# One column of table rows a tile of a graph network, fetched row by row by SyncE and ScalarE in place of one gather

## The reference

```python
for l in range(L):
    ht = einsum('nd,rdo->nro', h, W_rel[l])             # a row for each node and relation
    h_rel = segment_sum(ht[src, etype], dst) + h @ W_loop[l] + b_rel[l]
    z = (h @ W_gat[l]).reshape(n, H, DH)
    e = leaky_relu(sum(z * attn_l[l], -1)[src] + sum(z * attn_r[l], -1)[dst], 0.2)
    ex = exp(e - segment_max(e, dst)[dst])
    alpha = ex / segment_sum(ex, dst)[dst]
    h_gat = segment_sum(alpha[:, :, None] * z[src], dst).reshape(n, D) + b_gat[l]
    hc = concatenate([h_rel, h_gat], 1) @ W_fuse + b_fuse
    if l == 0: hc = hc * sigmoid(concatenate([hc, mean(edge_weight)], 1) @ W_gate + b_gate)
    h = relu(hc)
return layernorm(x + h)
```

## Time and profile before

| | |
|---|---|
| median of the runs (3959.73 to 3967.59) | 3964.04 us |
| span of the profiled execution, first to last instruction | 3490.2 us |
| GpSimd busy | 2489.3 us, 71% |
| VectorE busy | 2380.3 us, 68% |
| TensorE busy | 689.4 us, 20% |
| ScalarE busy | 424.8 us, 12% |
| mean DMA traffic | 145 GB/s |

### The profile page before, as it was taken

The page is one execution under the profiler, slowest core; times in us unless marked ns, Lnnn a source line. Parts: engine busy times, 40 slices in busy tenths (PEclk is TensorE's granted clock), DMA queues, the critical chain, the costliest instruction groups (busy, mean ns, idle before and its releaser), DMA issues.

```text
span 3490.2 us, 18122 instructions
## 1 busy us (share of the span) xinstructions
PE 689.4 (20%) x1897; PEld 372.5 (11%) x1897; DVE 2380.3 (68%) x3226; ACT 424.8 (12%) x769; POOL 2489.3 (71%) x2642
## 2 busy tenths in 40 slices
PE   8942111222122230011121111221000000000000
PEld 5421000111011110000000000110000000000000
DVE  8536666677676764665777756674776788877786
ACT  3530110111111120101111111111000000000000
POOL 1457777777777756777777777775777777777776
PEclk9965555555655555555555555555555555555555
DMA  7774444455545544444454544454433333333332
GB/s 271 315 249 129 134 147 152 152 151 152 152 152 159 168 145 118 130 151 152 151 152 151 153 152 152 152 173 140 107 106 107 107 106 107 106 106 107 106 103 74
DMA packets 143244, 505.96 MB, mean 145 GB/s; under 512 B 44277, under 2 KB 51002, under 8 KB 133618
## 3 DMA queue, kind: packets, MB, share of 16 engines
q0 software_dynamic: 130032, 444.45, 43.4%
q1 hardware_dynamic: 13186, 61.24, 4.5%
HBM read 341.05 MB, written 164.51 MB: 145 GB/s over the span
## 4 chain that ended last, share of the span: by engine, by line
POOL 45%; issue 29%; DVE 10%; DMA 6%; PE 4%; POOLq 3%; DVEq 1%; ACT 1%; SPq 1%; ACTq 0%
POOL meta_nat L594 20%; POOL late L594 14%; POOL scratch L594 10%; DVE acc L1381 3%; PE ps_table L886 1%; DMA late<-table,stage_mid 1%; DMA table<-rows 1%; DMA scratch<-table,stage_tail 1%; DVE late L1377 1%; DVE scratch L1377 1%; DVE meta_nat L1377 1%; POOLq L369 1%; POOL table L671 1%; DMA meta_nat<-table,stage_head 1%; PE ps_cnt L919 1%
## 5 line engine op out<-in xcount | busy, mean ns | idle before, releaser
L594 POOL DMA_INDIRECT meta_nat<-table,stage_head x1200 | 1139.0, 949 | 395.7 <-issue 385.3
L594 POOL DMA_INDIRECT late<-table,stage_mid x720 | 681.9, 947 | 219.4 <-issue 217.9
L594 POOL DMA_INDIRECT scratch<-table,stage_tail x555 | 525.9, 948 | 175.5 <-issue 175.2
L1025 PE MATMUL ps_mix<-ident,hr 128*128 128x128 f32 x75 | 35.5, 473 | 1991.2 <-DVE hg L1401 1991.2
L788 ACT ACTIVATE ps_cnt<-logit 128x68 f32<-128x68 f32 x189 | 43.7, 231 | 2767.1 <-DVE logit L1363 2766.1
L1381 DVE TENSOR_REDUCE acc<-meta_nat 128x132 f32<-128x2112 f32 x75 | 290.6, 3875 | 8.1 <-DVE meta_nat L1377 0.5
L1371 DVE TENSOR_REDUCE acc<-meta_nat 128x128 f32<-128x2048 f32 x75 | 282.6, 3767 | 0.0
L1049 PE MATMUL ps_table<-wrel,hT 128*128 128x512 f32 x400 | 266.4, 828 | 0.0
L1353 DVE TENSOR_TENSOR raw<-late,er_cur 128x64 f32<-128x64 f32 x45 | 12.0, 267 | 324.5 <-DMA late<-table,stage_mid 324.5
L1025 PEld LDWEIGHTS ps_mix<-ident,hr 128*128 128x128 f32 x75 | 13.6, 182 | 2039.8 <-DVE hg L1401 2039.8
L1381 DVE TENSOR_REDUCE acc<-scratch 128x132 f32<-128x1188 f32 (+1 forms) x69 | 208.7, 3024 | 7.1
(11 more groups left out here) (237 smaller groups left out, 1701.4 us busy)
## 6 DMA issues: line engine op xcount, KB each, us to landing
table<-rows SPq DMA_DIRECT2D x25, 2080.0 KB, 7.7
meta_nat<-table,stage_head POOLq DMA_INDIRECT x1200, 2.8
late<-table,stage_mid POOLq DMA_INDIRECT x720
scratch<-table,stage_tail POOLq DMA_INDIRECT x555, 2.8
meta<-meta_ranked SPq DMA_DIRECT2D x1, 2438.0 KB, 15.1
wrel<-in_L_gnn_W_rel POOLq DMA_DIRECT2D x2, 1024.0 KB, 13.5
meta_nat<-in_x SPq DMA_DIRECT2D x1, 832.0 KB, 18.4
table<-rows,stage_id POOLq DMA_INDIRECT x50, 7.8
```

Source lines behind the costliest of these rows:

```text
L594: pool.indirect_dma_start(out=slots[b][:, k, :], out_offset=None, in_=table[l % 2], in_offset=bass.IndirectOffsetOnAxis(ap=index, axis=0)) ...
L1025: pe.transpose(mix[0], hr[:], ident[:])
```

## The change

For tiles 1 to 24 of each layer the first column of the lists (the first edge of each node) is no longer gathered by GpSimd. The lists are 82 long; `M_LIST` is where GpSimd's own list starts, one behind `M_ELL`. `tile_slots` is one less for these tiles (16 at least), starts are one more and counts one less.

The first column of all tiles is transposed by TensorE, multiplied by 260, stored as `lone_rows` in HBM (25 x 128 integers). In each tile SyncE loads 80 of the 128 places into its part of SBUF and ScalarE 48. Each loads them into registers, 16 at a time, and issues for each one DMA of 1040 bytes from the table to one partition of `lone_row` [128, 260], with the address from the register. VectorE, at the start of a tile, waits for all of them, copies `lone_row` into slot 0 of buffer H, and signals (`s_taken`) that `lone_row` may be written again; both issuers wait for that signal before the next tile's rows. VectorE's head group then takes slots 0 to 16 as new edges. SyncE runs its own loop over the tiles. ScalarE issues its 48 in three chunks: after the gate, after the second group's exponential, and after the evacuations of the next table. The buffer `yo` is placed in the room of the relation weights.

```diff
+LIST = ELL + 2
-    SCATTERED = M_ELL + ELL
+    M_LIST = M_ELL + 1
+    SCATTERED = M_ELL + LIST
+    BY_SP = 80
+    BY_ACT = P - BY_SP
+    LOADED = 16
+        lone_rows = dram("lone_rows", [T, P], I32)
+        lone_row = sb("lone_row", [P, ROW])
+        def fetch_lone(eng, l, places, at, lanes, landed, regs):
+            eng.reg_load(regs, places[0:1, at:at + len(regs)])
+            for reg, p in zip(regs, lanes):
+                place = eng.snap(reg, min_val=0, max_val=NULL * ROW)
+                eng.dma_start(lone_row[p:p + 1, :], table_flat[l % 2][:, bass.ds(place, ROW)]
+                              ).then_inc(landed, 16)
...
+            def lone_tile(l, t):
+                sp.dma_start(lone_sp[:], lone_all[:, bass.ds(t * P, BY_SP)]
+                             ).then_inc(s_at_sp, 16)
+                sp.wait_ge(s_taken, n_taken)
+                sp.wait_ge(s_at_sp, n_at)
+                sp.reg_add(n_at, n_at, 16)
+                sp.reg_add(n_taken, n_taken, 1)
+                for c in range(0, BY_SP, LOADED):
+                    fetch_lone(sp, l, lone_sp, c, range(c, c + LOADED), s_lone_sp, regs)
...
+            for l in range(L):
+                if l:
+                    sp.wait_ge(s_stored, 16 * (1 + l * T))
+                with sp.Fori(1, T) as t:
+                    lone_tile(l, t)
...
+            def lone_chunk(l, c):
+                if c == 0:
+                    act.wait_ge(s_at_act, n_at)
+                    act.reg_add(n_at, n_at, 16)
+                    act.wait_ge(s_taken, n_taken)
+                    act.reg_add(n_taken, n_taken, 1)
+                fetch_lone(act, l, lone_act, c * LOADED,
+                           range(BY_SP + c * LOADED, BY_SP + (c + 1) * LOADED), s_lone_act, places)
...
+                if lone:
+                    if first and l:
+                        act.wait_ge(s_stored, 16 * (1 + l * T))
+                    lone_chunk(l, 0)
                 with act.If(groups > 1):
                     group()
+                    if lone:
+                        lone_chunk(l, 1)
                     with act.If(groups > 2):
                         group()
+                with act.Else():
+                    if lone:
+                        lone_chunk(l, 1)
                 if not first:
                     next_rows(l, act.snap(n_last, min_val=0, max_val=T - 1))
                     act.reg_add(n_last, n_last, 1)
+                if lone:
+                    lone_chunk(l, 2)
...
+            pe.wait_ge(s_lone, 1)
+            pe.transpose(ps_cnt[0:T, 256:256 + P], lone[:], ident[:]).then_inc(s_lone_ps, 1)
...
+            v.tensor_scalar(tile_slots[:, 1:T], tile_slots[:, 1:T], -1.0, float(PAIR), ALU.add, ALU.max
+                            ).then_inc(s_slots, 1)
...
+            def take_lone():
+                dve.wait_ge(s_lone_sp, n_lone_sp)
+                dve.wait_ge(s_lone_act, n_lone_act)
+                dve.reg_add(n_lone_sp, n_lone_sp, 16 * BY_SP)
+                dve.reg_add(n_lone_act, n_lone_act, 16 * BY_ACT)
+                v.tensor_copy(slots["H"][:, 0], lone_row[:]).then_inc(s_taken, 1)
+                dve.wait_ge(s_taken, n_took)
+                dve.reg_add(n_took, n_took, 1)
...
                 start_tile(l, t)
-                group("H", first=True, meanwhile=lambda: stage_next_head(t))
+                if not first:
+                    take_lone()
+                group("H", first=first, lone=not first, meanwhile=lambda: stage_next_head(t))
```

More of the change, by code:

```diff
@@ L57, in gnn_kernel @@
     CONSTS = 17
+    BY_SP = 80
+    BY_ACT = P - BY_SP
+    LOADED = 16
+    assert BY_SP % LOADED == 0 and BY_ACT % LOADED == 0
     ROUNDS = EC // (3 * HB)
@@ L171, in gnn_kernel @@
         assert CLS * T // 2 + 4 * 512 <= 3 * W
-        ell_valid = late[:, 6 * EC:6 * EC + T * ELL // 2].bitcast(BF16).rearrange("p (t j) -> p t j", t=T)
-        assert T * ELL // 2 <= 2 * EC
+        ell_valid = late[:, 6 * EC:6 * EC + T * LIST // 2].bitcast(BF16).rearrange("p (t j) -> p t j", t=T)
+        assert T * LIST % 2 == 0 and T * LIST // 2 <= 2 * EC
         in_tile = scratch[:, 0:T * T].rearrange("p (v t) -> p v t", t=T)
@@ L396, in hub_blocks @@
             return eng.snap(blocks, min_val=1, max_val=E // BLOCK), groups_of_block
+        table_flat = [table[i].rearrange("(o n) f -> o (n f)", o=1) for i in range(2)]
+        def fetch_lone(eng, l, places, at, lanes, landed, regs):
[4 more added lines that the diff above has]
+                              ).then_inc(landed, 16)
         block = ctx.enter_context(nc.Block())
@@ L824, in _, with lone_places, tile @@
             n_groups = counter(act, "act_groups", 0)
-            def tile(l, t, first=False):
+            places = [act.alloc_register(f"act_place{i}") for i in range(LOADED)]
+            n_at = counter(act, "act_at", 16)
+            n_taken = counter(act, "act_taken", 1)
+            lone_all = lone_rows.rearrange("(o t) p -> o (t p)", o=1)
+            def lone_places(t):
+                act.dma_start(lone_act[:], lone_all[:, bass.ds((t + 1) * P + BY_SP, BY_ACT)]
+                              ).then_inc(s_at_act, 16)
+            def lone_chunk(l, c):
[6 more added lines that the diff above has]
+                           range(BY_SP + c * LOADED, BY_SP + (c + 1) * LOADED), s_lone_act, places)
+            def tile(l, t, first=False, lone=True):
+                if lone:
+                    lone_places(t)
                 n = act.value_load(tile_slots[0:1, bass.ds(t, 1)], min_val=PAIR, max_val=E)
@@ L859, in _ @@
                 tile(l, 0, first=True)
-                with act.Fori(1, T) as t:
+                with act.Fori(1, T - 1) as t:
                     tile(l, t)
+                tile(l, T - 1, lone=False)
                 transposed(l)
@@ L1342, in stage_this_tail, with group @@
                     clear_tail(HALF)
-                at = dve.snap(in_first * PAIR + (t * META + M_ELL), min_val=0, max_val=(T + 1) * META - PAIR)
+                at = dve.snap(in_first * PAIR + (t * META + M_LIST), min_val=0, max_val=(T + 1) * META - PAIR)
                 v.tensor_copy(stage_tail[:], meta_flat[:, bass.ds(at, PAIR - 1)]).then_inc(s_tail, 1)
-            def group(b, first=False, meanwhile=None, K=PAIR):
+            def take_lone():
[6 more added lines that the diff above has]
+                dve.reg_add(n_took, n_took, 1)
+            def group(b, first=False, lone=False, meanwhile=None, K=PAIR):
                 lo = 1 if first else 0
+                new = 0 if lone else 1
                 dve.wait_ge(s_landed[b], n_land[b])
@@ L1366, in group @@
                 v.tensor_copy(leaky[:, 0:1], peak[:]).then_inc(s_keep, 1)
-                if not first:
+                if not (first or lone):
                     v.tensor_copy(slots[b][:, 0], acc[:]).then_inc(s_carried, 1)
```

81 lines of the change are left out of this document (59 added, 22 removed).

## The result

The changed kernel takes 5679.5 us in the median (5672.6 to 5684.6), the kernel before 3961.9 us; the ratio is 1.434, with a 95% interval of 1.432 to 1.437. I had said 4051 us and a range of 3885 to 4340. The sign was right; the loss was 1718 us for 87.

What follows compares the result with a forecast made beforehand. GpSimd's queue of indirect gathers, 1.25 us each, was taken to bound the kernel. With SyncE's loop at 41.8 us a tile, layers 0 and 1 lose 24.8 each and layer 2 37.4: 3964 + 87 = 4051 us, range 3885 to 4340.

Steps and rivals of the forecast that it cites:

- The 473.8 between them lies outside the span and stays.: Profiled span 3490.2 us against timed median 3964.0; the 473.8 us difference was taken as unchanged by the change.
- A fetch, d = 0.46: SyncE's queue: one single-row DMA with its address steps costs 0.46 us, so 80 rows take 36.8 us a tile.
- Five register loads, 1.6 us: SyncE's loop: five loads of 16 places a tile, each priced at 0.31 us from a one-value load on ScalarE.
- Landing and copy, 3.4 us: End of SyncE's turn: last row's landing 2.8 us, then VectorE's copy of lone_row with two semaphore hops 0.6.
- S = 41.8 us: Period of the loop of SyncE's fetches and VectorE's copy through lone_row; a tile lasts at least this long.
- Gain of tiles 1 to 11, -13.8; tiles 12 to 23, +38.6; layer 2, -12.5 and +49.9: Change in us: long tiles save a gather each, late ones wait for SyncE; layer 2 splits at tiles 10 and 11.
- Tile 24, nothing: Last tile of each layer: its saved gather counted as 0, since VectorE's, TensorE's and the store's tail follow it.
- ScalarE, 0: ScalarE's 48 fetches in three chunks of 7.7 us each, counted as 0 because SyncE's loop is already longer.
- All hidden: Rival: a fetch costs 0.367 us, SyncE's loop 34.4 us, fetching hidden; -73, so 3891 us; chance 0.36.
- Dearer issue: Rival: a fetch costs 0.545 us, SyncE's loop 48.6 us and sets most tiles; about +420, so 4380 us; chance 0.14.
- Code loaded again: Rival: SyncE's loop of about 250 instructions is reloaded each trip, period 44.2 us; +185, so 4149 us; chance 0.05.
- all slower cases: Whole kernel slower than before: forecast's own range 0.37, costlier fetch issue 0.14 and code reloading 0.05, together 0.56.

## Why the prediction failed, step by step

1. *"The 473.8 between them lies outside the span and stays."* This is the step that failed. It took a difference of 12% between a profile and the timed runs as a constant, and so did the sentence on it under the profile before. Where both come from one run they are 1.6 us apart, on either kind of chip. The 474 us lay inside the span, in a condition that the trace didn't contain: instructions of the queues held up while gathers are issued. (That all 474 are this is argued from the run without fetches.) The change puts 250 instructions a tile on SyncE and 150 on ScalarE into that condition, and the loss was 1718 us for 87. No row of the trace could price that; the gap itself could have told that the trace and the times weren't of one condition.
2. *A fetch, d = 0.46 (0.367 to 0.545).* Undisturbed 0.406, inside the bounds, though below the 0.42 under which I had called the forecast wrong; dearer loads and the store (3 and 5) made up for it. On the timed chip 2.5 us in the stretch with gathers and 0.5 in the one without. That is most of what lies between 3661 and 5680 us, of which 475 is what the kernel before loses already.
3. *Five register loads, 1.6 us.* 6.2 us. "Sixteen values may take longer; nothing here shows it" was true, and then the value for one was taken. The Trainium skill (Runtime: NRT & Kernel Launch, "Instruction fetch mechanics") gives about 200 ns a register even in bulk, for the runtime's own register loads, which come from HBM. If it held for these loads from SBUF too, one would be an estimated 3.2 us. The traces show less: 1.23 us for 16 values on SyncE and 0.28 for one on ScalarE, so some 63 ns for each further one.
4. *Landing and copy, 3.4 us.* The turn takes 3.95 over a row's pitch, with a register load in it, so 2.7 for the 3.4. That the load of the places lies beside landing and copy was right in layers 0 and 1, where it is done 0.1 to 0.3 us earlier; in layer 2 it ends last.
5. *S = 41.8 us.* 41.1 in layer 2, 44.9 in layers 0 and 1. A row 4.3 us cheaper and loads 4.6 dearer cancel; what is missing is 3.0 us of fetches slowed behind GpSimd's store, a term I didn't have.
6. *Gain of tiles 1 to 11, -13.8; tiles 12 to 23, +38.6; layer 2, -12.5 and +49.9.* On a 3486 chip -13.9, +73.6, -12.4 and +38.5. The +73.6 is 35 over the forecast, and 12 x 3.1 = 37 is what step 5 adds. Layer 2's is 11 under it: 13 x 0.7 = 9 since S is 41.1 there, the rest in tiles 12 to 14, which last 40.2, 40.1 and 39.1 us counted by GpSimd's starts. VectorE's copies are never less than 40.9 us apart there, but GpSimd starts its gathers ever further ahead of the copy, 22.5 us in tile 11 and 27.9 in tile 15; "a tile lasts max(GpSimd's work, S)" left that out. A gather saved is worth 13.9 / 11 = 1.26 us of GpSimd in a long tile, as the earlier trace rows had it. The rule weighed there, of the Trainium skill (DMA: Bandwidth & Descriptors, "Issuing engines are not separate DMA queues"), says that issuing from several engines saves only the time to initiate, usually small beside the DMA. Here that time is the 1.26 us, and beside the 2.8 us of a gather's landing it isn't small.
7. *Tile 24, nothing.* +12.6 and +12.2: its gathers are out after 27.5 us, but VectorE's copy still comes a full loop after the last.
8. *ScalarE, 0.* Right on a 3486 chip (3664 without it, 3661 with it), and right that it is the next limit (64 rows: 3710). Wrong on a 3960 chip: 48 rows alone cost 940 us over the run without fetches, and in the changed kernel VectorE waits 455 us at line 1495 for exponentials of ScalarE.
9. *Rivals.* "All hidden" is out, though the row at 0.406 was nearer to it than to my 0.46: with 0.286 a row and no register loads the loop was hidden (3427.6). "Dearer issue" is right that rows at SyncE set every tile on the 3960 chip, but no setup got dearer, and the tiles have no one length (94.7 us in tile 2 of layer 0, 60.9 in tile 23). "Code loaded again" is out: 35 packets on the instruction queue for 19, where 69 trips would need more, and on the 3486 chip no gap at a fixed place but at the register loads and the turn. Its price was also misread: the 1448 ns of the earlier trace rows isn't a first pass. GpSimd's first load took 306 ns, and the 12 loads of over 0.8 us stand in tiles 18 to 24 of layers 0 and 1. My chances gave all slower cases 0.56.

Against the kernel before of the same chip the forecast of +87 stands beside +174 (1.050) where the trace's condition held, and beside +1718 on the chip of the result. So half of the loss was missing even where the condition held: the fetches behind the store, and tile 24.

## What to carry over

Set the span of a profile against the timed runs first. If they are 12% apart, as here, the trace shows another condition, and every price read from it needs a second bound. Count instructions and not only microseconds when work moves to an idle queue: a loop that fetches 128 rows with some 400 instructions is exposed to anything that slows instructions, one gather hardly is. A loop through a single buffer must be summed with all its turns (the load of its places, register loads, the landing) and compared with the shortest tile, not the mean.

## What the runs showed of the hardware

- On three chips SyncE's queue let 0.7 to 1.1 instructions through in a us while GpSimd issued indirect gathers, whatever their kind, against 5.2 in the changed kernel on a 3486 chip. Single records are then up to 0.7 us long, and some 1.4: of a 17 ns semaphore step, a 29 ns MOVE, a 40 ns register step on VectorE. On two other chips the same steps kept 17, 29 and 40 ns. VectorE has 517 register and move steps over 0.4 us in the run without fetches and 4 in the changed kernel (counted from all records); why isn't shown. The kernel before takes 3961 to 3980 us on the first and 3486 on the second. A quarter of the gathers' bytes or of their rows doesn't change it (1.0 and 0.8); that their number does is only argued, since no run had fewer gathers with the same fetches. The slowness lasted 11 us past the last gather in the stretch shown. What makes a chip one or the other isn't known; it could be the chip, or its neighbours' work at that time, and the recording of instructions may have part in it.
- Undisturbed, a DMA of one 1040-byte row from SyncE costs 0.406 us of its queue with two address steps, from ScalarE 0.368; with a fixed address and no such steps SyncE's takes 0.286.
- A register load of 16 values from SBUF takes 1.23 us.
- Four DMAs of SyncE take 0.9 to 1.1 us each and not 0.23 just behind a store of 128 table rows by GpSimd. In layer 2, which has no such store, none does.
- A gather of 32 rows keeps GpSimd busy for 0.87 us, one of 128 rows for 0.95.
